# The router of a spiking attention and mixture-of-experts block: logits with tokens on the partitions

## The reference, cut to what matters

```python
# x: (2, 2048, 256) float32, 4096 tokens; 8 experts, 2 of them for a token
xn = layernorm(x)                          # no gain, no bias
attn = spiking_attention(xn)               # Q, K, V = spikes of layernorm(xn @ W.T + b)
logits = einsum('nh,eh->ne', xn, router_w) # (4096, 8)
probs = softmax(logits); scores, idx = top_k(probs, 2)
gate = scores / sum(scores), placed at idx
h = einsum('nh,ehd->end', xn, up_proj); hidden = silu(h[..., :256]) * h[..., 256:]
ffn = einsum('ne,enh->nh', gate, einsum('end,edh->enh', hidden, down_proj))
out = x + attn + ffn
```

## Time and profile before

| | us |
|---|---|
| median of 3 runs | 422.99 (421.54 to 424.07) |
| the profiled execution, its own time | 421.92 |
| its span, first to last instruction | 420.1 |
| TensorE busy (PE) | 367.0, 87% |
| VectorE busy | 270.8, 64% |
| GpSimd busy | 233.4, 56% |
| ScalarE busy | 225.8, 54% |
| mean granted clock of TensorE | 0.959 |

### The profile page before, as it was taken

How to read it: one execution, slowest core, us unless ns; L and a number is a source line. 1 busy time by engine, 2 the same in 40 slices (tenths; PEclk the granted TensorE clock), 3 DMA queues, 4 the chain that set the end, 5 groups by cost and what they waited for, 6 DMA issues and landing times.

```text
span 420.1 us, 9186 instructions
## 1 busy us (share of the span) xinstructions
PE 367.0 (87%) x2429; PEld 297.0 (71%) x2430; DVE 270.8 (64%) x897; ACT 225.8 (54%) x716; POOL 233.4 (56%) x207
## 2 busy tenths in 40 slices
PE   5198876999999989998979999999999999999980
PEld 1033676888888847665767888888888788888860
DVE  4699799987777646757775555555555555555540
ACT  1456774777777645534454555555555555555540
POOL 4547424777777753542335755464755555555652
PEclk9689978999999999998999999999999999999995
DMA  7943012244626323557455757565666656565643
GB/s 258 322 153 75 26 50 65 102 154 128 206 103 217 113 90 114 190 189 219 133 162 171 114 97 110 91 103 99 101 101 101 99 90 97 96 100 94 104 52 37
DMA packets 43460, 51.72 MB, mean 123 GB/s; under 512 B 6342, under 2 KB 37064, under 8 KB 43432
## 3 DMA queue, kind: packets, MB, share of 16 engines
q0 software_dynamic: 13952, 19.30, 26.2%
q1 hardware_dynamic: 27488, 30.21, 24.1%
q10 hardware_dynamic: 1992, 1.89, 1.4%
HBM read 27.89 MB, written 23.48 MB: 122 GB/s over the span
## 4 chain that ended last, share of the span: by engine, by line
PE 51%; DVE 19%; DMA 14%; ACT 6%; issue 5%; SPq 1%; POOLq 0%; DVEq 0%; POOL 0%; ACTq 0%
PE bank L1136 14%; PE bank L1138 13%; PE bank L1137 13%; DMA out<-xo 7%; DMA xn<-x 3%; PE bank L1278 3%; DVE qk_spk L1005 3%; PE bank L1260 3%; DVE xn L807 2%; DMA ew_f<-experts 2%; ACT junk L486 2%; DVE xst L785 2%; PE bank L1312 2%; DMA ex<-slot_x 2%; DVE exT_l L974 2%
## 5 line engine op out<-in xcount | busy, mean ns | idle before, releaser
L736 POOL DMA_INDIRECT out<-ey,dest x71 | 110.0, 1549 | 78.9 <-DMA out<-ey,dest 24.4
L1036 DVE TENSOR_TENSOR hid<-gact,bank 128x256 f32<-128x256 f32 x71 | 29.9, 421 | 76.7 <-ACT gact L531 76.7
L683 POOL DMA_INDIRECT slot_x<-xn,pos x64 | 62.8, 982 | 25.7 <-issue 19.3
L1136 PE MATMUL bank<-ew,exT_h 128*128 x142 | 62.1, 437 | 6.4 <-DVE exT_l L974 6.2
L1136 PE MATMUL bank<-w_h,xT_h 128*128 128x256 f32 x192 | 58.9, 307 | 0.3 <-DVE w_l L841 0.3
L531 ACT ACTIVATE gact<-bank 128x256 f32<-128x256 f32 x71 | 27.3, 384 | 57.2 <-PE bank L1138 57.2
L1137 PE MATMUL bank<-w_l,xT_h 128*128 128x256 f32 x192 | 56.3, 293 | 0.0
L1138 PE MATMUL bank<-w_h,xT_l 128*128 128x256 f32 x192 | 56.1, 292 | 0.0
L1138 PE MATMUL bank<-ew,exT_l 128*128 x142 | 55.9, 394 | 0.0
L1137 PE MATMUL bank<-ew,exT_h 128*128 x142 | 55.8, 393 | 0.0
L486 ACT ACTIVATE junk<-bank 128x256 bf16<-128x256 f32 x96 | 35.9, 380 | 27.7 <-PE bank L1138 27.4
(11 more groups left out here) (203 smaller groups left out, 893.3 us busy)
## 6 DMA issues: line engine op xcount, KB each, us to landing
ex<-slot_x SPq DMA_DIRECT2D x71, 130.0 KB, 2.6
ew_f<-experts SPq DMA_DIRECT2D x24, 256.0 KB, 3.2
xo<-x SPq DMA_DIRECT2D x16, 256.0 KB, 3.0
out<-xo SPq DMA_DIRECT2D x16, 256.0 KB, 3.5
xn<-x SPq DMA_DIRECT2D x6, 512.0 KB, 12.6
out<-ey,dest POOLq DMA_INDIRECT x71, 3.9
xn<-x SPq DMA_DIRECT2D x4, 256.0 KB, 3.8
w_f<-w_all ACTq DMA_DIRECT2D x1, 1024.0 KB, 8.1
```

The source lines that it names most:

```text
L683: pool.indirect_dma_start(slot_x, bass.IndirectOffsetOnAxis(ap=pos[:, k, t:t + 1], axis=0), xn[:, t, :], None).then_inc(s[done], 16)
L736: pool.indirect_dma_start(out, bass.IndirectOffsetOnAxis(ap=dest[:, j:j + 1], axis=0), ey[:, j % 4, :], None, compute_op=ALU.add).then_inc ...
L1036: v.tensor_tensor(hid[:, m % 2, :], gact[:, m % 2, :], h_ps[m % 2][:, F:2 * F], ALU.mult).then_inc(s["hid_done"], 1)
L1136: mm(dst, a_h, b_h, start=first, stop=False)
```

## The change

The router's matmul changes sides. Before, the router's weights (8 columns) were loaded and up to 512 tokens moved; now each tile's transposed tokens (128 columns) are loaded, in two halves of the contraction, and the 8 router columns move. The result has tokens on the partitions and is written straight into bank 7, where the choice reads it. The copies to lgT, their buffer, the 32 small transposes and three semaphores go; logits_done, counted once per group, takes their place.

```diff
--- before.py
+++ after.py
@@ -40,7 +40,7 @@
 OFFSETS = [0, 1, -1, 2, -2, 4, -4, 8, -8]
 WARM = 16
 POOL_PIECES = 8
-LGT_PIECE, BIAS_PIECE, RT_PIECE, XT_PIECE = 9, 13, 15, 17
+BIAS_PIECE, RT_PIECE, XT_PIECE = 13, 15, 17
 XT_TILES = NT - RG
 LEAD = 3
 RING = 4
@@ -134,8 +134,6 @@
         put = place_in(r_w)
         ew = put("ew", [P, PIECES, 2, PW], F32R)
 
-
-        lgT = place_in(r_w + LGT_PIECE * 2 * PW * 4)("lgT", [E, NT * P])
         put = place_in(r_w + BIAS_PIECE * 2 * PW * 4)
         bias_f = put("bias_f", [2, D])
         bias_h = put("bias_h", [2, D], F32R)
@@ -210,7 +208,6 @@
             return banks[bank][:, D * h:D * h + D]
 
         x_ps = [banks[i] for i in range(4)]
-        lgT_ps = [banks[4], banks[5]]
         lg_ps = banks[7]
         rank_ps = banks[7]
 
@@ -232,7 +229,7 @@
 
         names = """vec_in bias_in const_in router_in ident_in scale_in w_in small_in toep_in
             base_in w_based row0_gone ones_in pool_set ones_set two_set two_out two_back w_summed b_summed w_signed w_halved w_parted wo_parted b_signed b_halved bias_set
-            xstat_done xvar_done xrstd_done xn_done xs_ready x_turned xT_ready logitsT logitsT_set routed
+            xstat_done xvar_done xrstd_done xn_done xs_ready x_turned xT_ready logits_done
             chosen_set ranked gap_set gate_exp gates_set placed pads_placed pads_marked pads_done scattered
             q_turned xh_set xl_set qT_set proj_done ssq_done std_done heron spk_done kv_done
             piece_h piece_l pool_piece far_built far_set half_summed kv_set
@@ -404,10 +401,6 @@
                 nc.scalar.activation(where[:, at:at + 2, :, :].rearrange("p t c k -> p (t c k)"), x_ps[i % 4][:, :],
                                      ACT.Copy).then_inc(s["xT_ready"], 1)
 
-            def keep_lgT(g):
-                act.wait_ge(s["logitsT"], g + 1)
-                nc.scalar.activation(lgT[:, g * RG * P:(g + 1) * RG * P], lgT_ps[g % 2][0:E, :], ACT.Copy).then_inc(s["logitsT_set"], 1)
-
             def sum_weights(n):
 
                 c, g = n // G4, n % G4
@@ -439,8 +432,8 @@
 
             def piece_upper(n):
                 u = n % 2
-                if n == LGT_PIECE:
-                    act.wait_ge(s["routed"], 1)
+                if n == RT_PIECE:
+                    act.wait_ge(s["logits_done"], NT // RG)
                 if n == BIAS_PIECE:
                     act.wait_ge(s["bias_set"], 1)
                 if n >= XT_PIECE:
@@ -458,8 +451,6 @@
                 if g == NT // RG - 1:
                     halve_biases()
                     halve_weights(0)
-                if g >= 1:
-                    keep_lgT(g - 1)
                 if g == 1:
                     act.wait_ge(s["bias_in"], 32)
                     sum_biases()
@@ -468,7 +459,6 @@
                 if 2 <= g < 6:
                     piece_upper(g - 2)
             halve_weights(1)
-            keep_lgT(NT // RG - 1)
 
 
             def keep_qT(t, m):
@@ -646,7 +636,7 @@
                 g.tensor_tensor(w_f[:, c, 0:G3 * D], w_f[:, c, 0:G3 * D], w0_r[:, :], ALU.subtract).then_inc(s["w_based"], 1)
 
             def set_ones(group):
-                pool.wait_ge(s["logitsT"], group + 1)
+                pool.wait_ge(s["logits_done"], group + 1)
                 n = RG if (group + 1) * RG <= XT_TILES else RG // 2
                 for t in range(0, RG, n):
                     where, at = xT_part(group * RG + t)
@@ -856,7 +846,7 @@
             def over_e(col):
                 return col.unsqueeze(2).broadcast_to(all_te)
 
-            dve.wait_ge(s["routed"], 1)
+            dve.wait_ge(s["logits_done"], NT // RG)
             lg = lg_ps[:, 0:NT * E].rearrange("p (t e) -> p t e", e=E)
 
             def pick(logits, top, low, onehot):
@@ -1158,16 +1148,11 @@
 
             def logits(g):
                 pe.wait_ge(s["xT_ready"], 2 * (g + 1))
-                if g >= 2:
-                    pe.wait_ge(s["logitsT_set"], g - 1)
-
-                n = RG if (g + 1) * RG <= XT_TILES else RG // 2
-                for t in range(0, RG, n):
-                    where, at = xT_part(g * RG + t)
+                for t in range(RG * g, RG * (g + 1)):
+                    where, at = xT_part(t)
                     for c in range(KC):
-                        last = mm(lgT_ps[g % 2][0:E, t * P:(t + n) * P].rearrange("e (t k) -> e t k", k=P), w_rt[:, c, :],
-                                  where[:, at:at + n, c, :], start=(c == 0), stop=(c == KC - 1))
-                last.then_inc(s["logitsT"], 1)
+                        last = mm(lg_ps[:, t * E:(t + 1) * E], where[:, at, c, :], w_rt[:, c, :], start=(c == 0), stop=(c == KC - 1))
+                last.then_inc(s["logits_done"], 1)
 
             groups = NT // RG
             pe.wait_ge(s["router_in"], 16)
@@ -1177,12 +1162,6 @@
                 if g >= 1:
                     logits(g - 1)
             logits(groups - 1)
-
-            for t in range(NT):
-                if t % RG == 0:
-                    pe.wait_ge(s["logitsT_set"], t // RG + 1)
-                last = turn(lg_ps[:, t * E:(t + 1) * E], lgT[:, t * P:(t + 1) * P], id_f[0:E, 0:E])
-            last.then_inc(s["routed"], 1)
 
             def ranks():
```

## The result

The changed kernel takes 432.94 us (median of 4 runs, 431.9 to 433.68) against 423.38 (4 runs, 421.54 to 424.07): a ratio of 1.0231 with a 95% interval of 1.019 to 1.0272. It is 9.6 us slower. The forecast was 422.0 in a range of 419.8 to 425.2: wrong, in sign too. The profiled execution has a span of 431.6, against 420.1.

A forecast was written before the change was run, and what follows sets the result against it. ScalarE's queue was taken to hold up VectorE's choice, and everything behind it. Certain -0.96, possible -0.7 from the stall and +0.7 from the clock level gave -1.0: median 422.0 us, range 419.8 to 425.2.

The forecast's parts named there:

- The price of a record: TensorE's new router matmuls: 0.063 us a record at full clock, so 1.0 us a group, about 0.8 less than now.
- the sum: TensorE's front at the low level: 6 x 1.70 + 5 x 2.0 = 20.2 from 26.01, last transposes through at 46.2.
- none of it reaches the end: TensorE's router work stands beside VectorE's, so its small gain at full clock does not change the kernel's end.
- the slower rival: TensorE bounds the router stage, at low level and 0.215 a record 3.44 us a group: +8.7, 431.7; chance 0.12.
- The level: TensorE's clock: low for much of 20 to 50, costing 0 to +1.0 us; +0.7 taken.
- the other bound: Alternative price for TensorE's logits: the 128x128 transpose, about 0.107 us start to start, so 1.7 us a group.
- ScalarE's 0.96: Two lgT copies of 0.48 each leave ScalarE's series ahead of the router's choice: certain gain of 0.96 us.
- The stall of the first piece, 0.7: First expert piece rounded earlier, so GpSimd's subtraction no longer slows VectorE's column sum: possible gain of 0.7 us.
- Collisions in the choice: Expert pieces 4 and 5 on GpSimd can strike VectorE's choice differently, by one stall of 0.7 us either way.
- The first projections at the low level: TensorE's 36 records for tiles 0 and 1 take 7.7 us, ending at 57.3; at most some tenths late, covered by idle time.

The follow-up runs named there:

- e6_kick: Changed kernel with eight dense matmuls behind each of logits groups 0 and 1 only; 421.96 us, one run.
- e2_half: Changed kernel with only the first half of the router's contraction, 64 records instead of 128, logits incomplete; 421.37 us, ratio 0.995.
- e7_quiet_before: Kernel before, with the low parts of expert pieces 4 to 7 set to zero on GpSimd instead of subtracted; 419.08 us, ratio 0.9906.
- e8_quiet_last2: Kernel before, with the last two logits groups in the new form and low parts of expert pieces 4 to 7 zeroed; 419.77 us, ratio 0.9926.
- e12_late_kick: Changed kernel with eight dense matmuls behind logits groups 0 and 1, and expert pieces 4 to 7 moved to VectorE; 423.51 us, ratio 1.0013.
- e1_dense4: Changed kernel with four dense bf16 matmuls behind each of the first seven groups of logits; 426.89 us, ratio 1.0099.
- the best version: Kernel before, old router form, with low parts of expert pieces 4 to 7 moved from GpSimd to VectorE beside later projections; 420.18 us, ratio 0.9945.
- e9_idle: Changed kernel with 16 dense matmuls once, behind the transposes of group 0 in TensorE's pause; 434.18 us, ratio 1.0286.
- e4_iso: Kernel before with bursts of each matmul and transpose form behind its last matmul; fp32 matmul 0.11 us a record, fp32 transpose 0.06; kernel time not given.

## Why the prediction was wrong

- **The price of a record: the step that failed.** "I take 0.063, the row with the same counts of columns": the row was a transpose. A matmul of the same tiles takes 0.11 at the full level and 0.21 at the low one. A group at the low level was 3.4 us and not 2.0. Put into the sum as it stood, 6 x 1.70 + 5 x 3.44 from 26.0 gives 53.4 for the last transposes, where it had 46.2; they ended at 52.15, from a start 0.86 earlier. So TensorE became the bound of the front, and "none of it reaches the end" fell with the price. The number stood in the slower rival, with 0.12.
- **The level.** This half was right. The sum had the low level for all groups up to the last transposes, and it was low in all of them. It took both: at the full level the same records fit (e6_kick, the choice at 49.86), and at the low level half of them do (e2_half, 51.05). The argument against the rival, that the level would have to stay low all the time, was none: the sum itself counted so, and between 20 and 50 the trace of before shows the level rise only beside the 512-column matmuls that the change takes out.
- **What was at hand.** The right row was the other bound, the 128x128 transpose at 0.107, doubled at the low level; it was passed over for the shape. The rule of the Trainium skill (TensorE: Matmul & The Clock Gate, section LDWEIGHTS), by which a load takes its columns over 1.2 GHz whatever the rows, gives an estimate of 107 ns, and I let the transposes' row overrule it. At the full level 0.11 a record was measured, for 8 rows as for 128, as by the rule. At the low level it is twice that, which the rule's fixed 1.2 GHz doesn't give: followed to the letter it would have left a group at 1.7 us and the forecast as it was.
- **ScalarE's 0.96.** Right at its place (3.9 us for 4.9), hidden in the changed kernel, whose choice waits for TensorE; where it was laid bare (e7_quiet_before, e8_quiet_last2) it did not show in the median.
- **The stall of the first piece, 0.7.** Wrong. The cast still waited 1.08 us for the load and ran at 28.79; GpSimd's subtraction at 29.50 met the column sum at 29.91 (0.89 us) as before. VectorE's front ran 0.86 earlier in this execution (29.91 for 30.77), and the load did not come earlier with it. It is a matter of timing: in eight traces with the new form throughout, the sum took 0.17 (e6_kick, e12_late_kick) to 1.24 us (e1_dense4), in six with the old form there 0.87 to 1.08.
- **Collisions in the choice.** Called "0.7 either way"; in the changed kernel they cost 1.1 and 0.8 more than before, and one of them is the subtraction for wo_l, which the prediction doesn't have. In the best version their removal is worth more than all that the change could have gained.
- **The first projections at the low level.** Not on the path: TensorE's first 36 records ended at 64.5 and the choice at 66.6.
- **The slower rival.** +8.7 at the choice and at the end; measured +7.2 at its start (8.1 from a like start of the front), +9.1 at the first spikes, 9.6 in the median. The stalls add to what it counted. Its mechanism, place and size were right, and its chance too low.

## What to carry to other kernels

Swapping the sides of this small fp32 matmul left TensorE's own work as it was (1.7 us a group on either side, at the full level), but changed the clock at which all of its neighbours ran: look at the granted level before and ask which instructions were running when it rose. Price an operation from a row of the same operation and type, not from one with the same shape. And when a gain of an engine's queue doesn't show, look for the other engine's instruction that it has been moved beside.

## What the runs showed of the hardware

- 38 us of wholly busy TensorE (20.0 to 58.6), in fp32 transposes and fp32 matmuls with 8 moving columns, did not raise the level; dense bf16 matmuls on zeros among them did (e1_dense4), and so did the fp32 matmuls with 512 moving columns of the kernel before. Once full, it held through the same work for about 12 us (e6_kick) or 10 (e12_late_kick), and in e9_idle it fell about 1 us after a pause of 3.6.
- A 128x256 step of VectorE with two operands in SBUF (0.42 us) takes up to 1.5 us beside GpSimd's subtractions (1.52 at 70.68 in the changed kernel, beside two that take 2.70 together). Beside a memset of the same piece it lost little: the choice took 5.82 us in e7_quiet_before, 6.71 before.
- An fp32 matmul with 8 rows of weights costs as much as one with 128, 0.11 a record at the full level, and a bf16 one with 128 rows 0.024, with the same weights in each matmul of a burst (e4_iso).
